# Expert-choice stages: statistics, scaling and gate products of the tokens done another way

## The reference, cut to what matters

```python
hn = (tok - mean(tok)) / sqrt(var(tok) + 1e-5)      # each token over its 64 channels
logits = hn @ gate_w.T + gate_b                     # 32 experts
# per image and expert: softmax over all tokens, the 8 largest logits are its picks
pooled = sum_k prob[k] * hn[pick k]                 # 32 rows of 64 per image
out = gelu(pooled @ weight1[e] + b1[e]) @ weight2[e] + b2[e]
tok[pick k] += sum of prob * out over the experts that picked this token
```

## Time and profile before

| | us |
|---|---|
| median of 3 runs | 7054.31 |
| lowest and highest of them | 7049.75, 7062.92 |
| the profiled execution | 7050.06 |
| its span (first to last instruction) | 7048.0 |
| its mean granted TensorE clock | 0.87 of full speed |
| c0: from its first instruction to the start of MAX8 | 1296.3 to 1545.0 |
| c2: the same | 4383.8 to 4621.9 |

### The profile page before, as it was taken

The page is one execution under the profiler, slowest core; times in us unless marked ns, Lnnn a source line. Parts: engine busy times, 40 slices in busy tenths (PEclk is TensorE's granted clock), DMA queues, the critical chain, the costliest instruction groups (busy, mean ns, idle before and its releaser), DMA issues. The chain is left out here.

```text
span 7048.0 us, 133563 instructions
## 1 busy us (share of the span) xinstructions
PE 5467.1 (78%) x45760; PEld 3540.2 (50%) x45760; DVE 4366.0 (62%) x9000; ACT 3720.3 (53%) x6914; POOL 1471.2 (21%) x1358
## 2 busy tenths in 40 slices
PE   6776778663796777659996998730999999947787
PEld 4554555312453333349996998210555555523333
DVE  6665766567423778772223344669777777768786
ACT  5554556444544666462224322526767676746664
POOL 3333333434321000060000000423111111121110
PEclk9888888775898889859998999965999999968888
DMA  0111011222233777530000022224666666547666
GB/s 27 31 28 28 26 28 25 60 69 75 77 87 96 244 244 248 197 101 0 0 0 0 0 96 95 78 68 102 83 79 85 83 85 82 67 123 218 212 210 205
DMA packets 794194, 645.63 MB, mean 92 GB/s; under 512 B 496551, under 2 KB 644199, under 8 KB 793779
## 3 DMA queue, kind: packets, MB, share of 16 engines
q1 hardware_dynamic: 792755, 639.06, 37.0%
q0 software_dynamic: 1024, 1.05, 0.1%
HBM read 549.78 MB, written 90.20 MB: 91 GB/s over the span
## 5 line engine op out<-in xcount | busy, mean ns | idle before, releaser
L2332 PE MATMUL sw_pC<-sw_row,sw_wc 128*128 128x128 f32 x10160 | 1158.8, 274 | 56.2 <-DVE sw_row L2207 54.9
L2332 PEld LDWEIGHTS sw_pC<-sw_row,sw_wc 128*128 128x128 f32 x10160 | 1147.5, 191 | 58.2 <-DVE sw_row L2207 55.5
L2766 PE MATMUL sp_pC<-sp_work,sp_bands 64*64 64x512 f32 (+11 forms) x14592 | 985.7, 428 | 43.5 <-issue 43.5
L2195 DVE SCALAR_TENSOR_TENSOR sw_row<-sw_pC,sw_y 128x128 f32<-128x128 f32 x1016 | 337.4, 332 | 791.9 <-PE sw_pC L2332 791.9
L2766 PEld LDWEIGHTS sp_pC<-sp_work,sp_bands 64*64 64x64 f32 x14592 | 602.2, 133 | 430.3 <-issue 364.2
L2705 ACT ACTIVATE sp_pC<-sp_pC,sp_par 128x512 f32<-128x512 f32 x832 | 598.4, 741 | 371.0 <-PE sp_pC L2766 347.0
L1744 DVE TENSOR_TENSOR t_z<-t_z,t_ht 128x1024 f32<-128x1024 f32 x512 | 642.9, 1296 | 147.1 <-DMA t_z<-gate_rows 142.2
L2264 ACT ACTIVATE sw_y<-sw_row 128x128 f32 (+1 forms) x762 | 265.5, 348 | 592.3 <-DVE sw_row L2195 592.3
L1906 PE MATMUL t_pO<-t_z,t_ew 128*64 128x512 f32 x2048 | 549.2, 684 | 4.6 <-DVE t_z L1744 4.4
L2662 DVE TENSOR_TENSOR sp_work<-sp_work,sp_pC 128x512 f32<-128x512 f32 x512 | 351.2, 687 | 169.5 <-ACT sp_pC L2705 169.0
L1876 PE MATMUL t_pT<-t_ident,t_h 128*128 128x128 f32 x1024 | 194.3, 352 | 233.4 <-ACT t_gs L1803 129.3
(11 more groups left out here) (361 smaller groups left out, 10744.3 us busy)
## 6 DMA issues: line engine op xcount, KB each, us to landing
t_z<-gate_rows SPq DMA_DIRECT2D x512, 512.0 KB, 6.2
sp_bands<-windows SPq DMA_DIRECT2D x128, 512.0 KB
c_xs<-tokens SPq DMA_DIRECT2D x128, 256.0 KB, 2.6
cb_xs<-tokens SPq DMA_DIRECT2D x128, 256.0 KB, 2.8
wa_xs<-in_x SPq DMA_DIRECT2D x64, 256.0 KB, 2.8
tokens<-wa_xt SPq DMA_DIRECT2D x128, 128.0 KB, 2.3
tokens<-cb_h SPq DMA_DIRECT2D x64, 256.0 KB, 2.4
t_xs<-tokens SPq DMA_DIRECT2D x32, 512.0 KB, 9.0
```

What stands on the lines that cost most here:

```text
L2195: dve.scalar_tensor_tensor(row[par][c][:, :, PAD:PAD + P2], pC[c][:, 0:2 * P2].rearrange("p (b w) -> p b w", b=2), 0.0, line(sweep, c, i), ...
L2332: ins = pe.matmul(pC[c][:, 0:2 * P2], wc[:, sweep, m, :], row[1 - par][c][:, :, m:m + P2], start=(m == 0), stop=(m == 4))
L2766: ins = pe.matmul(out[halves[to], :, low * lo:low * hi], band[halves[k], (NV * g + j) % BANDS, q, AT[k][tap], :], v[halves[k], :, low * at ...
```

## The change

It rewrites the loop of `stage_choice_ffn` for both stages; what the function computes stays the same.

- **Statistics.** `total`, `mean`, `center`, `square` and `variance` are gone. DVE's `stats(t)` runs the statistics instruction `bn_stats` on each token (32 of them for the 4 images of a tile, 128 x 64 each) and puts the variance together from its result in four short operations on 128 x 32.
- **Mean.** It is taken out of the gate weights: DVE subtracts from each of the 32 gate rows its own mean, once, before the loop. A row that sums to zero gives the same product with a centred and an uncentred token.
- **Scaling in place.** DVE multiplies `xs` itself for images 0 to 2, ACT's `scale_last` that of image 3, in eight operations of 128 x 64. POOL has nothing left to do in the loop. `root` and the reciprocal are one operation each for a tile.
- **Gate products.** `gate_cols` is 128 x 32 with the same weights in both halves. m = 0 uses partitions 0 to 63 of `ht` and of the weights, m = 1 partitions 64 to 127. They write two different PSUM banks at the same 32 partitions.
- **Buffers.** `xs` is a ring of XR = 4 tiles (each with all four images) in the place of `spent`. There are two pairs of logits banks, `pL`, used by tiles in turn. A load waits for the transposes of the tile four before.
- **Order.** The loops are unrolled in full. SP loads tile 0 before the gate weights. POOL builds the identity and `first` ahead of the rest; the rest has a semaphore of its own, `tables_ready`. The work on `earlier`, `trashf` and `own_e` moves behind the pooled rows. ACT's order in a tile is `root` of the next tile, `scale_last`, then four `save`, with `save_logits` of the tile before after the second.

```diff
-            sp.wait_ge(zeros_ready, 1)
+            def load(t):
+                for b in range(B):
+                    if t >= XR:
+                        sp.wait_ge(h_turned, B * (t - XR) + b + 1)
+                    sp.dma_start(xs[:, t % XR, b, :, :].rearrange("p j c -> p (j c)"),
+                                 tok[b * S + t * TILE:b * S + (t + 1) * TILE, :].rearrange(
+                                     "(p j) c -> p (j c)", j=TS)).then_inc(x_in[t % XR], 16)
+
+            load(0)
             for p in range(2):
-                sp.dma_start(gate_rows[:, p, 64 * p:64 * p + 64], gate_w).then_inc(gate_in, 16)
+                sp.dma_start(gate_rows[:, p, :], gate_w).then_inc(gate_in, 16)
             for b in range(B):
                 sp.dma_start(gb[E * b:E * b + E, :], gate_b.rearrange("(e a) -> e a", a=1)).then_inc(gate_in, 16)
-            with sp.Fori(0, NT) as t:
-                for b in range(B):
-                    sp.wait_ge(centered, B * t + b + 1)
-                    sp.dma_start(xs[:, b, :, :], tok[bass.ds(b * S + t * TILE, TILE), :].rearrange(
-                        "(p j) c -> p j c", j=TS)).then_inc(x_in[b], 16)
+            for t in range(1, NT):
+                load(t)
...
+            dve.wait_ge(gate_in, 16 * NGATE)
+            link(dve.tensor_reduce(gate_mean[:, :], gate_rows[:, :, :], AX.X, ALU.add))
+            link(dve.tensor_scalar(gate_mean[:, :], gate_mean[:, :], 1.0 / C, None, ALU.mult))
+            dve.tensor_tensor(gate_rows[:, :, :], gate_rows[:, :, :], gate_mean[:, :].unsqueeze(2).to_broadcast([E, 2, C]),
+                              ALU.subtract).then_inc(gate_cut, 1)
+
+            def stats(t):
+                dve.wait_ge(x_in[t % XR], 16 * B * (t // XR + 1))
+                for b in range(B):
+                    for j in range(TS):
+                        ins = dve.bn_stats(bs[:, TS * b + j, :], xs[:, t % XR, b, j, :])
+                link(ins)
+                var = st[:, t % XR, :, :].rearrange("p b j -> p (b j)")
+                dve.tensor_tensor(rest[:, :], bs[:, :, 2], bs[:, :, 5], ALU.add)
+                link(dve.tensor_tensor(apart[:, :], bs[:, :, 1], bs[:, :, 4], ALU.subtract))
+                link(dve.scalar_tensor_tensor(var, apart[:, :], C / 4.0, apart[:, :], ALU.mult, ALU.mult))
+                dve.tensor_tensor(var, var, rest[:, :], ALU.add).then_inc(var_ready, 1)
+
+            def scale(t):
+                v = st[:, t % XR, :, :].rearrange("p b j -> p (b j)")
+                dve.wait_ge(std_ready, t + 1)
+                dve.reciprocal(v, v).then_inc(inverted, 1)
+                dve.wait_ge(inverted, t + 1)
+                for b in range(B - 1):
+                    x = xs[:, t % XR, b, :, :]
+                    dve.tensor_tensor(x, x, bcast(st[:, t % XR, b, :], TS), ALU.mult).then_inc(h_ready[b], 1)
+
+            stats(0)
             dve.wait_ge(gate_turned, 1)
...
+            dve.tensor_copy(gate_cols[:, :], pA[:, 0:E]).then_inc(gate_ready, 1)
+            stats(1)
+            for t in range(NT):
+                scale(t)
+                if t + 2 < NT:
+                    stats(t + 2)
+
+            dve.wait_ge(logits_saved, 2 * NT)
...
+            dve.wait_ge(tables_ready, 1)
...
+            dve.wait_ge(tables_ready, 1)
+            link(dve.tensor_copy(trashf[:, :], trash[:, :]))
+            link(dve.scalar_tensor_tensor(own_e[:, :], firstf[:, :], -float(E) / S, own_e[:, :], ALU.mult, ALU.add))
+            link(dve.tensor_copy(earlier[:, :, :], order[:, :, :]))
+            link(dve.tensor_scalar(earlier[:, :, :], earlier[:, :, :], own_e[:, 0:1], None, ALU.is_lt))
...
+            def root(t):
+                v = st[:, t % XR, :, :].rearrange("p b j -> p (b j)")
+                act.wait_ge(var_ready, t + 1)
+                act.activation(v, v, ACT.Sqrt, bias=eps[:, 0:1], scale=1.0 / C).then_inc(std_ready, 1)
+
+            def scale_last(t):
+                act.wait_ge(inverted, t + 1)
+                for j in range(TS):
+                    x = xs[:, t % XR, B - 1, j, :]
+                    ins = act.activation(x, x, ACT.Copy, scale=st[:, t % XR, B - 1, j:j + 1])
+                ins.then_inc(h_ready[B - 1], 1)
+
+            def save(n):
+                act.wait_ge(h_turned, n + 1)
+                if n >= 2:
+                    act.wait_ge(gates_ready, n - 1)
+                act.activation(ht[:, n % 2, :], pH[n % 2][:, :], ACT.Copy).then_inc(ht_saved, 1)
+
+            def save_logits(t):
+                act.wait_ge(gates_ready, B * t + B)
+                out = logits[:, t * TILE:(t + 1) * TILE].rearrange("q (p j m) -> q m j p", j=TS // 2, m=2)
                 for m in range(2):
-                    act.activation(out[:, m, :, :], pG[m][:, :].rearrange("q (j p) -> q j p", p=128), ACT.Identity,
+                    act.activation(out[:, m, :, :], pL[t % 2][m][:, :].rearrange("q (j p) -> q j p", p=128), ACT.Identity,
                                    bias=gb[:, 0:1]).then_inc(logits_saved, 1)
 
-            pipelined(act, NT, [(root, 1), (save_logits, -2), (square, 2), (save, -1)])
+            root(0)
+            for t in range(NT):
+                if t + 1 < NT:
+                    root(t + 1)
+                scale_last(t)
+                for b in range(B):
+                    save(B * t + b)
+                    if b == 1 and t > 0:
+                        save_logits(t - 1)
+            save_logits(NT - 1)
...
+            pe.wait_ge(gate_cut, 1)
+            pe.transpose(pA[:, 0:E], gate_rows[:, :, :].rearrange("e p c -> e (p c)"), ident[0:E, 0:E]).then_inc(gate_turned, 1)
             pe.wait_ge(gate_ready, 1)
-            pe.sem_inc(h_turned, 2)
-            pe.sem_inc(gates_ready, 1)
-            pe.sem_inc(ht_saved, 1)
-
-            def turn(t, b, n):
+
+            def turn(n):
+                t, b = n // B, n % B
                 pe.wait_ge(h_ready[b], t + 1)
+                if n >= 2:
+                    pe.wait_ge(ht_saved, n - 1)
+                for j in range(TS // 2):
+                    ins = pe.transpose(pH[n % 2][:, 128 * j:128 * j + 128],
+                                       xs[:, t % XR, b, 2 * j:2 * j + 2, :].rearrange("p j c -> p (j c)"), ident[:, :])
+                ins.then_inc(h_turned, 1)
+
+            def gates(n):
+                t, b = n // B, n % B
                 pe.wait_ge(ht_saved, n + 1)
-                for j in range(TS // 2):
-                    ins = pe.transpose(pH[b % 2][:, 128 * j:128 * j + 128],
-                                       h[:, b, 2 * j:2 * j + 2, :].rearrange("p j c -> p (j c)"), ident[:, :])
-                ins.then_inc(h_turned, 1)
-
-            def gates(t, b, n):
-                pe.wait_ge(ht_saved, n + 3)
-                if b == 0:
-                    pe.wait_ge(logits_saved, 2 * t + 1)
+                if b == 0 and t >= 2:
+                    pe.wait_ge(logits_saved, 2 * (t - 2) + 2)
                 for m in range(2):
-                    ins = pe.matmul(pG[m][E * b:E * b + E, :], gate_cols[:, m, :], ht[:, b % 2, :],
+                    half = slice(64 * m, 64 * m + 64)
+                    ins = pe.matmul(pL[t % 2][m][E * b:E * b + E, :], gate_cols[half, :], ht[half, n % 2, :],
                                     start=True, stop=True)
                 ins.then_inc(gates_ready, 1)
 
-            pipelined(pe, NT, [(turn, 0), (gates, -1)])
+            for n in range(B * NT):
+                turn(n)
+                if n > 0:
+                    gates(n - 1)
+            gates(B * NT - 1)
```

More of the change, by code:

```diff
@@ L697, in stage_choice_ffn @@
         eps = a.sb("eps", [128, 1])
-        gate_rows = a.sb("gate_rows", [E, 2, 128])
-        gate_cols = a.sb("gate_cols", [128, 2, E])
+        gate_rows = a.sb("gate_rows", [E, 2, C])
+        gate_mean = a.sb("gate_mean", [E, 2])
+        gate_cols = a.sb("gate_cols", [128, E])
         gb = a.sb("gb", [128, 1])
@@ L705, in stage_choice_ffn @@
         logits = a.sb("logits", [128, S])
[L706 to L709, removed]
+        bs = a.sb("bs", [128, B * TS, 6])
+        apart = a.sb("apart", [128, B * TS])
+        rest = a.sb("rest", [128, B * TS])
+        st = a.sb("st", [128, XR, B, TS])
         ht = a.sb("ht", [128, 2, 512])
@@ L751, in stage_choice_ffn @@
         act_done = a.sem("act_done")
-        zeros_ready = a.sem("zeros_ready")
         const_ready = a.sem("const_ready")
+        tables_ready = a.sem("tables_ready")
         gate_in = a.sem("gate_in")
         w_in = a.sem("w_in")
+        gate_cut = a.sem("gate_cut")
         gate_turned = a.sem("gate_turned")
         gate_ready = a.sem("gate_ready")
[L758 to L763, removed]
+        x_in = [a.sem(f"x_in{i}") for i in range(XR)]
         var_ready = a.sem("var_ready")
         std_ready = a.sem("std_ready")
+        inverted = a.sem("inverted")
         h_ready = [a.sem(f"h_ready{i}") for i in range(B)]
@@ L819, in _ @@
             link = Link(pool, pool_done)
[L821 to L825, removed]
```

(38 more changed lines are left out.)

27 lines of the change are left out of this document (3 added, 24 removed).

## The result

The changed kernel takes 6851.8 us (median of four, 6849.61 to 6859.88), the kernel before 7053.85 beside it: ratio 0.9714, with 0.9697 to 0.9731 as its 95% interval. 6845 was predicted.

What follows compares the result with a forecast made beforehand. PE was taken as the bound, with serial products, logits-bank handover and slow clock. At 7.5 us a tile, MAX8 at 17.6 + 14 x 7.5 + 16.2 = 138.8 us saves 109.9 + 99.3 = 209, giving 6845; 8-in-10 range 6820 to 6905.

Steps and rivals of the forecast that it cites:

- Products: PE's two gate products per step run side by side: 1.83 us becomes 0.91 + 0.05, a step 1.55, a tile 6.2.
- DVE: DVE's statistics, four short operations, reciprocal and three scalings sum to 7.2 to 7.3 us a tile.
- rival 2: PE's clock stays low in the loops: 11.6 us a tile, 6960 us in all; chance 0.06.
- ACT: ACT's root, eight scalings, four saves and two logit copies sum to 6.7 to 7.0 us a tile.
- rival 1: ACT or PE in lockstep, or costly statistics: 8.5 to 9.7 us a tile, 6873 to 6907 us; chance 0.2.
- Transfers: Tile loads and stores: 1 MB a tile at 140 GB/s, half of the engines' time, hidden.
- rival 3: The ring of tile loads runs in series: 18.0 us a tile, 7139 us, 1.2% slower; chance 0.02.
- Beginning: Stage start: small loads, gate means, statistics of tiles 0 and 1, reciprocal; scaling of tile 0 starts at 17.6 us.
- End: From the start of tile 14's scaling to MAX8: ACT's last work, last products and last logits, 16.2 us.
- Moved work: Some 2.9 us of DVE work behind the pooled rows, hidden by its wait for PE, which shrinks from 8.19 to 5.3.
- the handover of the only pair of logits banks: Old loop: PE idle 2.70 us a tile around ACT's logit copy, part of a tile of about 14 us.
- idle time with no releaser: Sign that the prediction is wrong: engines idle in the unrolled code with nothing shown as ending the wait; no size given.

Runs made afterwards that it cites:

- e1_serial: Changed kernel with gate products on all 128 rows again, weights zero in the other half: 6942.2 us, ratio 0.9832.
- e7_stats_first: Changed kernel with 34 idle ACT increments in either expert-choice stage and DVE's statistics of tile 0 ahead of the gate means: 6833.6 us, ratio 0.9679.
- u2_pairs: Kernel before with its expert-choice loops unrolled and a second pair of logits banks, products as before: 7047.7 us, ratio 0.9982.
- u4_late: Kernel before, unrolled, with halves side by side, two pairs of logits banks and ACT's logit copy two steps later: 6958.0 us, ratio 0.9856.
- e6_before_pad: Kernel before with 222 idle semaphore increments in ACT's queue in either expert-choice stage: 7083.1 us, ratio 1.0029.
- e5_pad34: Changed kernel with 34 idle semaphore increments in ACT's queue in either expert-choice stage: 6835.6 us, ratio 0.968.
- e2_one_pair: Changed kernel with one pair of logits banks for all tiles: 6972.6 us, ratio 0.9875.
- u1_halves: Kernel before with its expert-choice loops unrolled and the gate products on 64 rows each: 6982.3 us, ratio 0.9886.

## Why the prediction was right, point by point

- **Products.** 1.55 a step was predicted, 1.56 measured; four records take 1.05 in place of 1.90. The added change of mode, against which I set up to 0.12 us a step, is not seen.
- **DVE.** 7.2 to 7.3 a tile was predicted and 7.08 measured; from start to start in the timeline above, 1.81 for the scalings, 4.18 for the statistics, 0.71 for the four short operations and 0.38 for the reciprocal. The 0.2 for falls of the clock was not needed, since the clock stays at 1.00; with it falls rival 2. (That rival's 11.6 us a tile takes 1.45 a step where the prediction's own step is 1.55; with 1.55 it would have been 12.4 and 6982.) So 7.5 was 0.4 too much, which is 28 x 0.4 = 12 us.
- **ACT.** 6.7 to 7.0 predicted; 72.5 of 80 us is 6.4 a tile. It doesn't hold DVE in the loop, where no DVE row waits for ACT; rival 1 falls. e1_serial is that rival made real: 9.7 a tile, and the DVE wait for ACT that it foresaw, although the two tiles of statistics lay ahead there too.
- **Transfers.** 155 GB/s at 0.54 of the engines' time, half as predicted, and no wait on `x_in` in the loop; rival 3 falls.
- **Beginning.** 17.6 us to the first scaling was predicted, and it is 1320.29 - 1301.18 = 19.1. The gate operands land at 6.7 (1307.85 - 1301.18) instead of 6.0, and the gate means, priced at 0.8, take 2.2 (to 1310.09); statistics took 0.6 less than priced. The timeline after:

```profile
1307.77 2.06 POOL L837 IOTA c_order<- 128x2048 int32 x1
...
1308.15 1.70 DVE L860 TENSOR_SCALAR c_gate_mean<-c_gate_mean 32x2 f32<-32x2 f32 x1
...
1320.29 1.89 DVE L883 TENSOR_TENSOR c_spent<-c_spent,c_st 128x512 f32<-128x512 f32 x3
```

  A 32x2 operation takes 1.70 us while POOL writes its table; in e7_stats_first, with POOL done, 0.16.
- **End.** 16.2 predicted, 16.4 measured, from the scaling of tile 14 to MAX8. The wait behind it is ACT's last copy:

```profile
1419.44 1.90 DVE L883 TENSOR_TENSOR c_spent<-c_spent,c_st 128x512 f32<-128x512 f32 x3
...
1435.82 17.23 DVE L895 MAX8 c_top<-c_logits 128x8 f32<-128x16384 f32 x1 [12.29 <-ACT c_logits L996]
```

  19.1 + 14 x 7.08 + 16.4 is 134.6, so the form of the sum held, and MAX8 comes 4.1 to 4.2 us earlier than predicted.
- **Moved work.** Hidden, as said: the wait of 8.19 in the earlier trace rows became 4.18, where 5.3 was predicted.

```profile
1503.82 0.69 DVE L955 TENSOR_TENSOR c_mine<-c_pG,c_own 128x512 f32<-128x512 f32 x1 [4.18 <-PE c_pG L1076]
```

- **What bounded the kernel before.** Here a step of the prediction was wrong though its number was right. I put 2.7 of the 14 us down to "the handover of the only pair of logits banks". u2_pairs gave a second pair and kept the hole: PE's idle 2.5 us before `ht` and the slow products of 3.28 us. What u4_late showed in its place is ACT's copy standing right behind the products that it waits for, worth some 12 us a stage when moved; what the rest of the hole came from wasn't taken apart. The sum didn't suffer, because I priced the loop after from its new queues and not as the old loop less the handover.
- **What the sum lacked.** It had no term for stages that the change doesn't touch. The two stages gave 218.5 us where 209 was predicted; the top-2 stages took some 16 to 23 back. So 6845 against 6851.8 is closer than the steps deserve: two misses of about 10 and 20 us have opposite signs. I did name idle time with no releaser as a sign against the prediction, but looked for it in the unrolled code. It came where a later loop jumps back.

The parts, in us of MAX8 of c0: 248.7 before; 239.6 unrolled; 209 with halves; 197 with the late copy and the pair; 134.6 with statistics, scaling and order of the change.

## What to carry to other kernels

A wait shows the instruction that ended it, not why that was late, so look at what stands ahead of it in its engine's queue before calling a buffer the cause. Price a new loop from what each engine has to do in a tile, with its beginning and end apart. Where code is written out, look at the loops behind it on each engine for idle time with no releaser, and move them by a few idle instructions.

## What the runs showed of the hardware

- Instruction supply: a loop on ACT pays 3.4 to 6.2 us at each of three jumps back in the first top-2 stage (after, e6_before_pad), or nothing that is seen (before, e5_pad34), by its place in the code; in the second top-2 stage every kernel has three waits of some 2 to 4 us, and after and e6_before_pad a fourth. On this kernel that is 16 us one way and 22 the other. That 34 and 222 instructions decide it is shown, and that instructions are loaded during the waits; where exactly the boundary lies isn't.
- DVE and POOL at once: a 128x512 scaling takes some 0.63 in a row of three alone and 1.07 beside POOL, whose own takes 1.55; a 32x2 operation takes 1.70 beside POOL's table of 128x2048 and 0.16 without it.
- TensorE: two products over 64 rows each, on different rows of the array and into different banks, run at the same time in full (1.05 us for what takes 1.90); a price for the change of mode twice a step isn't seen (a step is 1.56, and 1.55 was summed without one).
- The clock: at 1.00 in the changed kernel, where PE is busy for 6.4 of 7.08 us and idles for at most 0.67; 0.80 in e2_one_pair, where one idle piece a tile is 2.78 us, and products behind it take 1.82 in place of 1.05. But u1_halves is at 1.00 with PE busy for only 38.9 of 70 us (longest idle piece 1.6), and u4_late at 0.90 with 46.6 of 70 (longest 1.3). So the busy share doesn't order these runs, and what sets the clock between them isn't shown.
